# Older chunks first in three pipelined passes of a graph network, and half a copy less in its sort

## The chip, the cores and the metric

One core of a Trainium2 chip runs the whole program. The metric is the device time of one execution in microseconds (us); lower is better.

## The reference, cut to what matters

Two graph layers run over 100,000 nodes of 64 features and 25,000 edges (src, dst; sorted by dst). Between them and before them stands a layer norm. The second one has three rounds:

```python
for l in range(3):
    f1 = relu(x[row] @ nb_W[l] + nb_b[l])
    f2 = relu(x[col] @ self_W[l] + self_b[l])
    h = relu(concatenate([f1, f2], axis=1) @ att1_W[l] + att1_b[l])
    log_alpha = (h @ att2_W[l] + att2_b[l])[:, 0]
    mask = clip(sigmoid(log_alpha) * (ZETA - GAMMA) + GAMMA, 0.0, 1.0)
    rowsum = segment_sum(mask, row, num_segments=n) + 1e-06
    d_inv_sqrt = clip(rowsum ** (-0.5), 0.0, 10.0)
    vals = mask * d_inv_sqrt[row] * d_inv_sqrt[col]
    x = segment_sum(vals[:, None] * x[col], row, num_segments=n)
    out = out + x
```

Here row is src, col is dst, and x is the features of the nodes. The kernel needs the edges sorted by src as well, and so sorts 32,768 keys (two lists of edge ends, padded) itself.

## The kernel before, in words

**The sort** comes first. VectorE holds 128 x 512 keys and does a bitonic sort in 15 rounds. Each step is an `exchange`: one min (L1706) and one max (L1707) of 128x256 elements, from one buffer into the other. Rounds 9 to 15 also compare across partitions: TensorE turns the keys into a PSUM bank, VectorE copies all 512 columns back (L1716), exchanges, TensorE turns them again, and VectorE copies all 512 again (L1722). There are 14 such copies. Nothing else of the kernel can start before the sorted keys are stored.

**The second layer** works on 49 chunks of 512 edge slots, in three rounds (`l` = 0, 1, 2). Each round has first a pass that computes the attention of every edge and ends in the row sums, here called pass 1, 2 and 3, and then an aggregation. In a pass each chunk goes through these operations, on two engines whose queues run in program order:

- TensorE: turn (L1509 in pass 1, L1513 later), m1 (two products, L1523 and L1524), m2 (L1531, L1532), m3 (L1537), each waiting for ScalarE's result before it
- ScalarE: fill (copies of what was turned, L1431 and L1432), e2 (two Relus, L1437 and L1438), e3 (one Relu, L1445)

A helper, `staged`, writes the order out: at index i it calls each function for chunk i minus its lag, in the order of its list. After the pass ScalarE takes one sigmoid of 98x256 (L1449), VectorE works out the row sums (from L1313 on), and ScalarE takes a square root (L1451).

*Pass 1* has more in it. GpSimd (POOL) gathers both end rows of every edge by eight indirect DMAs a chunk (L1076) into two buffers; a buffer is free again once VectorE has passed `h_base`, at the end of the layer norm of the chunk that was in it. VectorE's norm of a chunk is: sum and centre (L570, L572), a square on ScalarE (L587), sum (L576), a root on ScalarE (L591), and scaling (L582, L1214). The square and the root are the first things in ScalarE's `fill` of this pass. Beside that, chunks 0 to 36 carry lookups: VectorE makes a one-hot (`above`, L1251), TensorE multiplies (`seek`, four groups of three L1490 and one L1492), VectorE selects the result of the lookup before (`found`, L1259). Every third chunk (2, 5, 8, ...) carries two lookups, the others one. `seek` is the last item in TensorE's list. At chunk 37 VectorE does a long piece, `place`.

*Passes 2 and 3* gather four rows a chunk (L1096). In them VectorE and ScalarE also take one step per chunk of a dense layer norm over all nodes (RUN_B, RUN_C): ScalarE's part is a square (L410) and a root (L415), VectorE's begins with L394, and SyncE loads and stores its rows. In the first 25 chunks VectorE also does two scans a chunk (L1239). After pass 3 VectorE waits until the last dense rows are stored (`run_stored`), and only then looks at the sigmoid. SyncE waits for the same stores at the end of `run_sp`, before it loads rows for the aggregation (`spread`, L1151).

Of the kernel before, what the change touches and what calls it, by code (L numbers as in the profile page):

```python
# [9 lines left out]
ALU = mybir.AluOpType  # L10
ACT = mybir.ActivationFunctionType
# [3 lines left out]
P = 128  # L15
# [31 lines left out]
NC1 = T1 // C  # L47
# [42 lines left out]
def build(nc, a, out):  # L90
    ctx = ExitStack()
    with ctx:
        def sb(name, shape, dt=F32):
            return ctx.enter_context(nc.sbuf_tensor(name, shape, dt))
# [168 lines left out]
        steps = sb("steps", [P, 256])  # L263
        row_of = sb("row_of", [P, 1])
        one_c = sb("one_c", [P, 1])
        perm1 = VAL1[:, :].bitcast(I32)
        rise = sb("rise", [RB1, 256])
        starts = sb("starts", [RB1, 1])
# [191 lines left out]
        def run_sp(sp, tag, src, dst):  # L460

            for c in range(DEPTH - 1):
                run_load(sp, tag, src, c)
            for c in range(len(tag[1])):
                run_store(sp, tag, dst, c)
                if c + DEPTH - 1 < len(tag[1]):
                    run_load(sp, tag, src, c + DEPTH - 1)
            run_stored(sp, tag)

        def run_stored(eng, tag):  # L470
            n = len(tag[1])
# [642 lines left out]
        def L1_sp(sp):  # L1114
# [31 lines left out]
            for l in range(LAYERS):  # L1146
                def spread(j, l=l):
                    b, c = j % 2, LOOKUPS[l][j]
                    if l or j >= 2:
                        sp.wait_ge(signal("o_hot"), LOOKUPS_BEFORE[l] + j - 1)  # L1150
                    sp.dma_start(RB[b], row_d[:, C * P * c:C * P * (c + 1)].broadcast_to([P, C * P])).then_inc(signal(f"o_ids{b}"), 16)  # L1151

                def store(c, l=l):
                    sp.wait_ge(signal("q_out"), l * NC1 + c + 1)
                    sp.dma_start(sums_of(xt_d[l], c), TS[:, c % 2]).then_inc(signal(f"q_stored{c % 2}"), 16)

                def load(c):
                    b = c % 3
                    if c >= 3:
                        sp.wait_ge(signal("q2_fin"), c - 2)  # L1160
                    sp.dma_start(LR[b][0].rearrange("p k f -> p (k f)"), base_d[c]).then_inc(signal(f"q2_ld{b}"), 16)
                    for n_ in range(2):
                        sp.dma_start(LR[b][1 + n_], sums_of(xt_d[n_], c)).then_inc(signal(f"q2_ld{b}"), 16)
                if l < 2:
                    for j in range(2):
                        spread(j)
                    sp.wait_ge(signal("r_val"), l + 1)
                    for h in range(2):
                        sp.dma_start(at(degree_d, 256 * h, [[512, COLS // 2], [1, 256]]), DEGR[h * (COLS // 2):(h + 1) * (COLS // 2)]).then_inc(signal("degrees_out"), 16)
                    due = looked_at(l, 3)  # L1170
                    staged(NC1, [(0, lambda i: [spread(j) for j in due(i) if j >= 2]), (5, store)])
                    for b in range(2):
                        sp.wait_ge(signal(f"q_stored{b}"), 16 * len(range(b, NC1, 2)) * (l + 1))
                    sp.sem_inc(signal("table"), 1)
                    run_sp(sp, (RUN_B, RUN_C)[l], x1_d, out)
                else:
                    for b in range(2):
                        sp.wait_ge(signal(f"h_stored{b}"), 16 * len(range(b, NC1, 2)))
                    staged(NC1, [(0, spread), (2, load)])

        def L1_dve(v):
            v.wait_ge(signal("x1_fixed"), 1)
# [46 lines left out]
            for l in range(LAYERS):  # L1229
                rowsum_dve(v, l)  # L1230
                aggregate_dve(v, l)
                if l < 2:
                    v.wait_ge(signal("s_bt"), NC1 * (l + 1))
                    v.wait_ge(signal("q_out"), NC1 * (l + 1))
                    for i in range(NC1):
# [3 lines left out]
                            v.tensor_tensor_scan(ownT[:, lo:hi][:, ::-1], sameB[:, lo + 1:hi + 1][:, ::-1], ownT[:, lo:hi][:, ::-1],  # L1239
                                                 ownT[:, hi:hi + 1] if c < NC1 - 1 else 0.0, ALU.mult, ALU.max).then_inc(signal("h_own"), 1)  # L1240
                        run_step(v, (RUN_B, RUN_C)[l], i)
                if l == 1:
                    run_stored(v, RUN_B)
                    run_stored(v, RUN_C)

        def above(v, e):

# [169 lines left out]
        def L1_act(s_):  # L1417

            for l in range(LAYERS):
# [24 lines left out]
                        s_.wait_ge(signal("h_m3"), l * NC1 + i - 1)  # L1444
                    s_.activation(HH[b], bank[4 + tb(l, i)][:, 0:256], ACT.Relu, bias=bias2[:, l:l + 1]).then_inc(signal("h_e3"), 1)  # L1445
                dense = [(0, lambda i, l=l: run_act_step(s_, (RUN_B, RUN_C)[l - 1], i))] if l else []
                staged(NC1, [(0, fill), (1, e2), (2, e3), *dense])
                s_.wait_ge(signal("h_m3"), (l + 1) * NC1)
                s_.activation(MR, bank[6][0:RB1, 0:256], ACT.Sigmoid, bias=bias3[0:RB1, l:l + 1]).then_inc(signal("r_sig"), 1)  # L1449
                s_.wait_ge(signal("r_total"), l + 1)  # L1450
# [20 lines left out]
        def L1_pe(pe):  # L1471
# [27 lines left out]
            for l in range(LAYERS):  # L1499
# [37 lines left out]
                    pe.matmul(bank[6][0:RB1, 0:256], at2[:, l, 48 - c:48 - c + RB1], HH[i % 2], start=(i == 0), stop=(i == NC1 - 1)).then_inc(signal("h_m3"), 1)  # L1537
                if l:
                    pe.wait_ge(signal("q_out"), l * NC1)
                staged(NC1, [(0, turn), (1, m1), (2, m2), (3, m3), *([] if l else [(0, seek)])])  # L1540

                pe.wait_ge(signal("r_ends"), l + 1)
                pe.matmul(bank[7][0:1, 0:RB1], PF[:, 255:256], ident[0:RB1, 0:RB1], start=True, stop=True)
# [102 lines left out]
        def _(v):  # L1646
# [55 lines left out]
            def exchange(cur, oth, d):  # L1702
# [4 lines left out]
                v.tensor_tensor(y[:, :, 1, :], x[:, :, 0, :], x[:, :, 1, :], ALU.max)  # L1707
                return oth, cur

            turns = 0  # L1710
            for k in range(1, 16):
                if k >= 9:
                    v.drain().then_inc(signal("turn_in"), 1)
                    turns += 1
                    v.wait_ge(signal("turned"), 2 * turns - 1)
                    v.tensor_copy(cur, bank[0][:, :])  # L1716
                    for st in range(k - 9, -1, -1):
                        cur, oth = exchange(cur, oth, 1 << st)
                    mid_side.append(0 if cur is KA else 1)
                    v.drain().then_inc(signal("turn_in"), 1)  # L1720
                    v.wait_ge(signal("turned"), 2 * turns)
                    v.tensor_copy(cur, bank[1][:, :])  # L1722
                for st in range(min(k, 8) - 1, -1, -1):
                    cur, oth = exchange(cur, oth, 1 << st)
                end_side.append(0 if cur is KA else 1)
                v.drain()
# [306 lines left out]
```

## Time and profile before

| | us |
|---|---|
| median of 3 executions (2831.07 to 2831.59) | 2831.31 |
| the profiled execution, device time | 2831.4 |
| its span, first to last instruction | 2829.6 |
| DVE (VectorE) busy | 2091.3 (74%) |
| POOL (GpSimd) busy | 1905.7 (67%) |
| PE (TensorE) busy | 1649.0 (58%) |
| ACT (ScalarE) busy | 1073.2 (38%) |
| mean granted TensorE clock | 0.768 of full |

Busy shares are averages over stages with different limits, so the stage of each edit has to be read by itself. The profiled execution lasts 1.8 us longer than its span, for what lies before the first instruction and after the last.

### The profile page before, as it was taken

How to read it: one execution, taken by the hardware profiler on the slowest of the kernel's cores; microseconds unless marked ns; L12 is line 12 of the kernel's file. 1: busy time of each engine (PE TensorE's matmuls, PEld its weight loads, DVE VectorE, ACT ScalarE, POOL GpSimd, SP SyncE). 2: the span in 40 equal slices, each digit the busy share in tenths (PEclk: the TensorE clock that was granted, in tenths of full speed). 3: DMA queues.
4: the chain of work that ended last, by engine and by line, in shares of the span. 5: the costliest groups of instructions: out<-in, count | busy, mean ns of one | idle time of the engine just before them, and what ended most of it. 6: DMA issues, size and time to landing. Idle time of an engine off the chain costs nothing.

```text
span 2829.6 us, 32874 instructions
## 1 busy us (share of the span) xinstructions
PE 1649.0 (58%) x8788; PEld 1262.0 (45%) x8788; DVE 2091.3 (74%) x5660; ACT 1073.2 (38%) x2214; POOL 1905.7 (67%) x1896
## 2 busy tenths in 40 slices
PE   1135667676508888256666546746666655656663
PEld 0025666666405555145454334534444444434442
DVE  6766998899778999355655536979668889657775
ACT  0025666666304443033333334434444344442221
POOL 0037777777786766677777774767766477745776
PEclk9997877877558888577777767878888778876555
DMA  0023444444201111422222112333323333324443
GB/s 8 0 60 92 137 129 138 129 139 127 84 2 32 45 43 41 87 59 66 61 62 64 41 35 56 85 99 105 103 91 74 86 102 105 104 68 120 126 116 81
DMA packets 279791, 226.66 MB, mean 80 GB/s; under 512 B 161731, under 2 KB 209855, under 8 KB 279481
## 3 DMA queue, kind: packets, MB, share of 16 engines
q1 hardware_dynamic: 221113, 184.48, 23.1%
q0 software_dynamic: 58496, 40.08, 6.8%
q8 instruction: 74, 1.21, 0.2%
q14 instruction: 108, 0.88, 0.1%
HBM read 151.81 MB, written 84.50 MB: 84 GB/s over the span
## 4 chain that ended last, share of the span: by engine, by line
POOL 48%; DVE 18%; issue 18%; PE 7%; DVEq 6%; DMA 2%; SPq 1%; ACT 1%; POOLq 0%; ACTq 0%
POOL big L1096 14%; POOL G L1076 13%; POOL regs L1973 7%; POOL out L1103 7%; POOL regs L1982 6%; DVE den L1377 2%; DVE big L1706 2%; PE bank L1562 2%; DVE bank L836 2%; DVE big L1394 2%; DVEq L1705 1%; PE bank L994 1%; DVE bank L847 1%; DVE G L830 1%; DVEq L837 1%
## 5 line engine op out<-in xcount | busy, mean ns | idle before, releaser
L1096 POOL DMA_INDIRECT big<-layer_rows,late x392 | 401.0, 1023 | 152.0 <-issue 118.8
L1973 POOL DMA_INDIRECT regs<-in_x,G x200 | 202.2, 1011 | 234.8 <-DVEq L1825 174.2
L1562 PE MATMUL bank<-regs,SQ 99*128 99x256 bf16 x1308 | 228.7, 345 | 84.7 <-ACT SQ L1467 78.1
L1103 POOL DMA_INDIRECT out<-G,scat_i x196 | 195.7, 999 | 104.3 <-issue 61.6
L1982 POOL DMA_INDIRECT regs<-in_x,G x200 | 220.1, 1101 | 65.4 <-issue 60.3
L685 POOL DMA_INDIRECT x_after_layer<-big,scat_i x200 | 196.5, 983 | 84.3 <-issue 65.7
L1076 POOL DMA_INDIRECT G<-x_after_layer,own_i x196 | 199.9, 1020 | 70.2 <-issue 60.7
L1076 POOL DMA_INDIRECT G<-x_after_layer,far_i x196 | 197.8, 1009 | 65.8 <-issue 65.8
L1064 POOL DMA_INDIRECT late<-degree_factors,late x152 | 152.8, 1005 | 99.9 <-DMA degree_factors<-den 56.6
L1562 PEld LDWEIGHTS bank<-regs,SQ 99*128 99x128 bf16 x1308 | 153.9, 121 | 144.7 <-ACT SQ L1467 97.0
L439 PE MATMUL bank<-regs 128*128 128x128 f32 x784 | 135.9, 327 | 119.4 <-DVE den L397 118.7
L1377 DVE SCALAR_TENSOR_TENSOR den<-steps,late,bank 128x256 f32<-128x256 f32 x436 | 182.0, 473 | 10.0 <-PE bank L1562 10.0
L439 PEld LDWEIGHTS bank<-regs 128*128 128x128 f32 x784 | 117.3, 230 | 135.4 <-issue 134.4
L1513 PE MATMUL bank<-ident,big 128*128 128x128 f32 x196 | 48.5, 337 | 217.4 <-DMA big<-layer_rows,late 217.4
L1509 PE MATMUL bank<-ident,XC 128*128 128x128 f32 x196 | 48.8, 398 | 211.1 <-DVEq L1215 211.1
L1465 ACT ACTIVATE SQ<-XC,row_of 128x512 bf16<-128x512 bf16 x109 | 78.4, 719 | 222.9 <-DMA XC<-row_of_far_degree 166.7
L587 ACT ACTIVATE SQ<-XC 128x512 f32<-128x512 f32 x99 | 62.3, 629 | 261.8 <-DVE XC L572 261.7
L527 PE MATMUL bank<-regs 128*128 128x196 bf16 x800 | 130.0, 307 | 27.6 <-DVE regs L543 24.2
L1997 POOL DMA_INDIRECT farf<-dst_float,VAL x96 | 122.4, 1275 | 29.2 <-issue 29.2
L1513 PEld LDWEIGHTS bank<-ident,big 128*128 128x128 f32 x196 | 22.5, 161 | 261.4 <-issue 261.4
L1509 PEld LDWEIGHTS bank<-ident,XC 128*128 128x128 f32 x196 | 32.1, 201 | 223.1 <-issue 223.1
L1524 PE MATMUL bank<-den,regs 128*128 128x256 f32 x294 | 127.4, 528 | 0.0
(417 smaller groups left out, 5384.6 us busy)
## 6 DMA issues: line engine op xcount, KB each, us to landing
den<-in_x SPq DMA_DIRECT2D x96, 256.0 KB, 3.7
x_after_layer<-den SPq DMA_DIRECT2D x96, 256.0 KB, 2.1
regs<-x_after_layer SPq DMA_DIRECT2D x96, 256.0 KB, 2.8
out<-regs SPq DMA_DIRECT2D x96, 256.0 KB, 2.1
XC<-row_of_far_degree SPq DMA_DIRECT2D x109, 128.0 KB
layer_rows<-TS SPq DMA_DIRECT2D x98, 128.0 KB
regs<-sought SPq DMA_DIRECT2D x49, 196.0 KB
regs<-row_of_edge SPq DMA_DIRECT2D x75, 128.0 KB
```

What stands on the lines that cost most here:

```text
L439: ins = pe.matmul(bank[(3, 6)[d % 2]][:, q * P:(q + 1) * P], XT[d % 2][:, q * P:(q + 1) * P], CM, start=True, stop=True)
L527: pe.matmul(o_, GE[b][h][:, k * P:(k + 1) * P], LT[:, h, part, :], start=(h + part == 0), stop=False)
L685: g.indirect_dma_start(x1_d, bass.IndirectOffsetOnAxis(ap=scat_i[0][:, u:u + 1], axis=0), big2[:, u, :], None, bounds_check=top, oob_is_er ...
L1064: g.indirect_dma_start(DCc[:, u:u + 1], None, degree_d, bass.IndirectOffsetOnAxis(ap=pos_i[:, u:u + 1], axis=0), bounds_check=top, oob_is_ ...
L1076: g.indirect_dma_start(G[:, b, grp // 2, grp % 2, :], None, x1_d, bass.IndirectOffsetOnAxis(ap=ix[:, u:u + 1], axis=0), bounds_check=top, ...
L1096: ahead(g, l, REVERSED, lambda u, l=l: g.indirect_dma_start(far[:, tile_of(u // C, u % C), :], None, xt_d[l - 1], bass.IndirectOffsetOnAxi ...
L1103: g.indirect_dma_start(out, bass.IndirectOffsetOnAxis(ap=scat_i[1][:, u:u + 1], axis=0), SUM[b][:, k, :], None, bounds_check=top, oob_is_e ...
L1377: v.scalar_tensor_tensor(PICK[k], steps[:, :], far_c[:, u:u + 1], bank[2 + 2 * (j % 2) + k // 2][:, (k % 2) * 256:(k % 2) * 256 + 256], AL ...
L1524: pe.matmul(bank[2 + b][:, 256:512], wb[:, 1, l, :], FT[b], start=True, stop=True).then_inc(signal("h_m1"), 1)
L1562: ins = pe.matmul(bank[2 + 2 * b + k // 2][:, (k % 2) * 256:(k % 2) * 256 + 256], OH[b][0:RB1 + 1, k * P:(k + 1) * P], TAB[0:RB1 + 1, part ...
L1973: g.indirect_dma_start(GR[:, c % DEEP, k, 0, :], None, a["x"], bass.IndirectOffsetOnAxis(ap=own0[:, c * C + k:c * C + k + 1], axis=0), bou ...
L1982: g.indirect_dma_start(GR[:, c % DEEP, k, 1, :], None, a["x"], bass.IndirectOffsetOnAxis(ap=far0[:, c * C + k:c * C + k + 1], axis=0), bou ...
```

## The change

Four edits. In the sort only the upper half of each turned pair is copied; the lower half is read by min and max in the PSUM bank. In the three passes TensorE's list becomes m3, m2, m1, turn and ScalarE's e3, e2 (in passes 2 and 3 then the dense step), fill; the lookup stays last on TensorE. At the last chunk ScalarE does a sigmoid on one column, so that the table for it is loaded there; in pass 1 after the fill, in passes 2 and 3 before it. VectorE's wait for the dense stores goes, and SyncE's moves behind the first two `spread` loads of the next aggregation.

```diff
@@ run_sp
                 if c + DEPTH - 1 < len(tag[1]):
                     run_load(sp, tag, src, c + DEPTH - 1)
-            run_stored(sp, tag)
@@ L1_sp
+                for j in range(2):
+                    spread(j)
+                if l:
+                    run_stored(sp, (RUN_B, RUN_C)[l - 1])
                 if l < 2:
-                    for j in range(2):
-                        spread(j)
...
-                    staged(NC1, [(0, spread), (2, load)])
+                    staged(NC1, [(0, lambda j: spread(j) if j >= 2 else None), (2, load)])
@@ L1_dve
-                if l == 1:
-                    run_stored(v, RUN_B)
-                    run_stored(v, RUN_C)
@@ L1_act
-                staged(NC1, [(0, fill), (1, e2), (2, e3), *dense])
+
+                def warm(i):
+                    if i == NC1 - 1:
+                        s_.activation(warm_c[:, :], one_c[:, :], ACT.Sigmoid)
+                staged(NC1, [(2, e3), (1, e2), *dense, *([(0, warm), (0, fill)] if l else [(0, fill), (0, warm)])])
@@ L1_pe
-                staged(NC1, [(0, turn), (1, m1), (2, m2), (3, m3), *([] if l else [(0, seek)])])
+                staged(NC1, [(3, m3), (2, m2), (1, m1), (0, turn), *([] if l else [(0, seek)])])
@@ block.vector, the sort
+            def exchange_turned(turned, cur, oth, d):
+                t_ = turned.rearrange("p (g t d) -> p g t d", t=2, d=d)
+                x = cur.rearrange("p (g t d) -> p g t d", t=2, d=d)
+                y = oth.rearrange("p (g t d) -> p g t d", t=2, d=d)
+                v.tensor_copy(x[:, :, 1, :], t_[:, :, 1, :])
+                v.drain()
+                v.tensor_tensor(y[:, :, 0, :], t_[:, :, 0, :], x[:, :, 1, :], ALU.min)
+                v.tensor_tensor(y[:, :, 1, :], t_[:, :, 0, :], x[:, :, 1, :], ALU.max)
+                return oth, cur
...
-                    v.tensor_copy(cur, bank[0][:, :])
-                    for st in range(k - 9, -1, -1):
+                    cur, oth = exchange_turned(bank[0][:, :], cur, oth, 1 << (k - 9))
+                    for st in range(k - 10, -1, -1):
...
-                    v.tensor_copy(cur, bank[1][:, :])
-                for st in range(min(k, 8) - 1, -1, -1):
+                    cur, oth = exchange_turned(bank[1][:, :], cur, oth, 1 << 7)
+                for st in range((min(k, 8) if k < 9 else 7) - 1, -1, -1):
```

## Rows read from the trace of the kernel before

**Rows 1.** The page's chain that ended last, shares of the span by source line.

```profile
POOL big L1096 14%; POOL G L1076 13%; POOL regs L1973 7%; POOL out L1103 7%; POOL regs L1982 6%; DVE den L1377 2%; DVE big L1706 2%; PE bank L1562 2%; DVE bank L836 2%; DVE big L1394 2%; DVEq L1705 1%; PE bank L994 1%; DVE bank L847 1%; DVE G L830 1%; DVEq L837 1%
```

**Rows 2.** Waits of POOL, 1185 to 1710 us (pass 1): total us, times, longest.

```profile
POOL G L1076 <- issue: 120.0, 374, 2.6
```

**Rows 3.** Timeline, pass 1: turns of chunks 0, 3, 37: start us, length us, what.

```profile
1191.55 1.09 PE L1509 MATMUL bank<-ident,XC 128*128 128x128 f32 x4 [6.01 <-DVEq L1215]
...
1220.93 0.75 PE L1509 MATMUL bank<-ident,XC 128*128 128x128 f32 x4 [3.87 <-DVEq L1215]
...
1582.50 0.63 PE L1509 MATMUL bank<-ident,XC 128*128 128x128 f32 x4 [3.59 <-DVEq L1215]
```

**Rows 4.** Timeline, pass 1: one step with two lookups (chunk 11) and the next turn.

```profile
1304.83 1.08 PE L1509 MATMUL bank<-ident,XC 128*128 128x128 f32 x4 [3.63 <-DVEq L1215]
...
1305.70 1.06 PE L1523 MATMUL bank<-big,regs 128*128 128x256 f32 x2
...
1306.05 0.08 DVE L1259 DVE_READ_ACCUMULATOR regs<-bank,late,steps 128x1 f32 x1
...
1307.66 0.47 ACT L1437 ACTIVATE den<-bank,bias 128x256 f32<-128x256 f32 x1 [1.05 <-PE bank L1524]
...
1312.53 0.69 DVE L570 TENSOR_REDUCE stat<-G 128x8 f32<-128x512 f32 x1
...
1314.03 0.63 ACT L587 ACTIVATE SQ<-XC 128x512 f32<-128x512 f32 x1 [4.19 <-DVE XC L572]
...
1317.41 1.09 PE L1509 MATMUL bank<-ident,XC 128*128 128x128 f32 x4 [3.87 <-DVEq L1215]
```

**Rows 5.** Stretch 1190 to 1320 us: engines' busy us, then granted clock, DMA share, GB/s.

```profile
1190.00:1320.00 130.00, 80.91 (x415) 63.79 (x416) 75.51 (x220) 39.09 (x95) 99.11 (x97) 0.72 0.26 66
```

**Rows 6.** Timeline, PE, pass 1: low clock in a lookup, twice; the earliest rise.

```profile
1192.43 0.84 PE L1490 MATMUL bank<-regs 98*128 98x256 bf16 x3
...
1418.49 0.84 PE L1490 MATMUL bank<-regs 98*128 98x256 bf16 x3
...
1490.80 0.69 PE L1531 MATMUL bank<-den,regs 128*128 128x256 f32 x2
```

**Rows 7.** Timeline, end of pass 1: from the last chunk's turn to the sigmoid's table.

```profile
1700.98 1.09 PE L1509 MATMUL bank<-ident,XC 128*128 128x128 f32 x4 [5.25 <-DVEq L1215]
...
1706.07 0.60 PE L1523 MATMUL bank<-big,regs 128*128 128x256 f32 x2
...
1706.94 0.60 PE L1531 MATMUL bank<-den,regs 128*128 128x256 f32 x2
1707.14 0.47 ACT L1437 ACTIVATE den<-bank,bias 128x256 f32<-128x256 f32 x1 [1.15 <-PE bank L1524]
...
1707.51 0.47 ACT L1438 ACTIVATE den<-bank,bias 128x256 f32<-128x256 f32 x1
...
1709.56 1.40 PE L1537 MATMUL bank<-den,regs 128*98 128x256 f32 x4
1709.76 0.47 ACT L1445 ACTIVATE den<-bank,bias 128x256 f32<-128x256 f32 x1 [1.28 <-PE bank L1532]
1710.25 1.28 ACT L1449 ACT_TABLE_LOAD   x1
```

**Rows 8.** Timeline, end of pass 3: last turn, sigmoid, first VectorE row behind its wait.

```profile
2522.43 0.41 PE L1513 MATMUL bank<-ident,big 128*128 128x128 f32 x2 [0.89 <-DMA big<-layer_rows,late]
...
2529.84 0.47 ACT L1449 ACTIVATE den<-bank,bias 98x256 f32<-98x256 f32 x1
...
2534.76 0.29 DVE L1313 TENSOR_SCALAR den<-den 98x256 f32<-98x256 f32 x1 [7.72 <-DMA out<-regs]
```

**Rows 9.** Groups of VectorE by shape: 512 copied out of a bank; 256 added from one.

```profile
L853 DVE TENSOR_TENSOR big<-bank,big 128x256 f32<-128x256 f32 x50 | 20.4, 408 | 1.8 <-PE bank L1003 1.8
...
L1716 DVE COPY big<-bank 128x512 f32<-128x512 f32 x7 | 4.8, 692 | 8.7 <-PE bank L1914 8.7
```

**Rows 10.** Waits of all engines, 1990 to 2112 us (second half of pass 2).

```profile
DVE bank L394 <- ACT dstat L415: 34.7, 24, 3.1
```

More of the change, by code:

```diff
@@ L265, in build @@
         one_c = sb("one_c", [P, 1])
+        warm_c = sb("warm_c", [P, 1])
         perm1 = VAL1[:, :].bitcast(I32)
```

## The prediction

> **What bounds the kernel now.** I read the page first, for the chain that ended last [rows 1]. GpSimd's indirect DMAs head it, one line per stage; the 13% of L1076 are pass 1. So I asked stage by stage whether GpSimd is ever held up. In pass 1 it is not: 374 of its idle stretches are the 0.32 us between two issues [rows 2]. Then I read the timeline of pass 1, step by step. From the turn of chunk 3 to that of chunk 37 there are 34 steps in 361.6 us, 10.63 us each [rows 3], which is the pace of eight gathers. Last I read the three ends of the passes and the sort, where no gather runs and each microsecond counts in full.
>
> **The sort.** Each of 14 full copies from a bank takes 0.69 us [rows 9]. A 256-wide operation that reads a bank takes 0.41 us, so I price the half copy at that: 0.28 us less. The min and max now read one operand in the bank; 0.41 us for such an add [rows 9] says that this costs nothing. The sort has no cover and nothing beside it, so 14 x 0.28 = **-3.9 us**. Bounds: 0, if reading the bank made min and max slower by as much together, and 14 x 0.35 = 4.9 if a half copy took half.
>
> **The end of pass 1.** Before: the last turn starts at 1700.98, then come m1, m2, m3 of chunks 47, 46, 45, and only then m1 of 48 at 1706.07; the sigmoid is ready to start at 1711.5, behind its table load [rows 7]. New: the turn is followed by m3 of 46, m2 of 47 and m1 of 48. At the low clock m3 takes 0.85 and m1 and m2 1.71 each, twice the 0.87 from L1523 to L1531 at the high one [rows 7]. So m1 of 48 starts at 1704.4. The low clock lasts until about 1706. L1437 starts 1.96 us after L1523 at the low clock [rows 4], 1.07 at the high one [rows 7]: 1706.4. e2 takes 0.84 (L1437 start to L1438 end), m2 to e3 1.07, e3 0.47, and m3 after e3 0.73 (1710.96 minus 1710.23) [rows 7]. That gives 1709.5 for the sigmoid: **-2.0 us**. The table load (1.28 us, rows 7) now lies between fill and e3 of 47, where ScalarE waits for m2 until 1704.7.
>
> **The end of pass 2** has the same rows as pass 3 and no wait of VectorE; the same count gives **-1.6 us**. Its load lies before the last fill. It is covered if ScalarE's dense step 48 is done 1.6 us (load and one column) before the last gather lands. Now VectorE waits for ScalarE in 24 steps of the second half of pass 2 [rows 10], since that dense step stands behind e3, which hangs on the gather; in the new order it comes right after e2 of the chunk before, so I expect it to be early. Without cover it costs up to 2.1 us.
>
> **The end of pass 3.** The last turn is at 2522.43 and the sigmoid at 2529.84, but VectorE starts at 2534.76, since it waits for the store [rows 8]. New, by the same terms and all at the high clock: m3, m2 and m1 of 48 start at 2522.7, 2523.1, 2524.0; L1437 2525.1, end of e2 2525.9, e3 2527.0, m3, sigmoid 2528.2, VectorE 2528.7. That is **-6.0 us**. SyncE's wait for the stores stays, but its first final load comes only after ScalarE's first one-hot, some 9 us later, so nothing new is late.
>
> On table loads the Trainium skill ("ScalarE: Activation LUTs", What ACT_TABLE_LOAD costs) gives 2.66 us a switch, drain included. The trace shows 1.28 us and then the sigmoid. By the page's figure the gains at the ends would still hold, as the loads are covered either way.
>
> **Pass 1 under the new order.** This is where I expect the loss. ScalarE's queue now has e3 and e2 ahead of fill, and fill begins with the norm's square for the chunk that has just landed. e2 of chunk c waits for m1 of c, and in TensorE's queue m1 of c stands behind m3, m2, and these behind the lookup of chunk c. Before, all this came after the fill, and the lookup behind everything. So now a closed loop runs from turn to turn: turn, lookup, m3, m2, m1, e2, square, rest of the norm, next turn. If it is longer than 10.63 us, GpSimd waits for `h_base`.
>
> Its terms, from the turn's start: the lookup starts when VectorE has the first half of the result before, at 1306.13 minus 1304.83 = 1.3, plus 0.15, so 1.45. A lookup is four groups; at the low clock one takes 0.69 (four end 2.8 us after the first start, of which rows 6 have one), at the high one 0.35. m3 and m2 before m1: 2.56 low, 1.30 high. From m1's start to the square: 1.07 + 0.86 = 1.93 high, 2.82 low. From the square to the next turn: 1317.41 minus 1314.03 = 3.38 [rows 4].
>
> The granted clock in this stretch is 0.72 [rows 5]: 1.2 GHz in part of each step, 2.4 in the rest. In the 34 steps it rose between 2.7 us (L1531 at 1490.80, turn at 1488.21) and 5.9 us (L1490 still low at 1418.49, turn at 1413.34) after the turn [rows 6], 4.35 in the mean. TensorE idles about as long per step in the new order (4.4 us against 3.9), so I keep this mean. One lookup: 1.45 + 2.76 = 4.21, then m3 and m2 almost all at the high clock, m1 at 5.6, square at 7.5, **10.9 us**. Two lookups: the halves of the first end at 2.8 and 4.2, and VectorE's selection takes 0.8 for each, until 5.1; the second half of the second lookup waits for that, starts at 5.25 and ends at 5.95, m1 at 7.25, square at 9.2, **12.55 us**. The old step with two lookups took as long, 12.58 [rows 4], since VectorE started L570 only at 7.7; but the steps with one made it good again, and now they can't.
>
> Sum over the 34 steps: 23 x 10.9 + 11 x 12.55 = 388.8, against 361.6: +27.2. At the start, chunk 1 has no gather to wait for: its lookup starts 0.88 us after the turn [rows 3, 6], ends at 3.65, m1 follows at the low clock (2.82) and then the 3.38, so its turn comes 9.85 us after chunk 0's at 1191.55; then 10.9 and 12.55 give 1224.85 for chunk 3, against 1220.93: +3.9. GpSimd is 4.3 us ahead of the loop at most, and `place` at chunk 37, during which it already is held up a little, takes that slack away. So **+31 us**, carried to the end. Chunks 38 to 48 have no lookup; their loop is at most 9.6 us and hides.
>
> A rule of the skill speaks the same way ("TensorE: Matmul & The Clock Gate", Step-by-step: what each phase is for): matmuls stay in program order. Were it otherwise, m1 could pass a lookup and the gathers would still set the pace.
>
> **Passes 2 and 3 in the middle.** The loop fill, m1, e2, dense square and root, fill is 0.4 + 1.96 + 0.84 + 0.9 = 4.1 us at the low clock, under the four gathers' 5.3. Nothing.
>
> **The sum**, against the profiled execution's 2831.4 (the median is 2831.3): -3.9 - 2.0 - 1.6 - 6.0 + 31 = +17.5, so 2849.
>
> **The rivals.**
> - *The loop hides* (0.22). If TensorE were at the high clock all through, one lookup gives 9.4 us and two 11.5, 30.3 for three steps against 31.9 of gathers, and only the gains are left: 2818. With the earliest rise everywhere (10.15, 12.05) three steps take 32.35 and it is about 2826. The point that decides is 31.9 us for three steps. Against it: the clock was low at the start of nearly every step, with the same idle time before it.
> - *The dense steps hold up the fill in passes 2 and 3 too* (0.08). In the first half VectorE's step has two scans more and goes at about the gathers' pace. If ScalarE waited in each of 98 steps 0.3 us more than the gathers allow, that is 29 us more: 2878.
> - *The sigmoid's table does not stay* (0.04). If each Relu behind it needed another, three loads of 1.28 us come in at each end, and the gains there shrink by some 4 us: 2853. Now Relu and Copy run after Exp and after Sqrt without one.
>
> **How the numbers follow.** The forecast (0.66) is 2849, its own range 2836 to 2864: a mean rise half a microsecond earlier or later moves a step by 0.25 to 0.3 us, the sum by 10. The range of 8 in 10 has to take in the first rival: 2817 to 2864. A difference under 0.2%, 5.7 us, can't be told from none here. Slower: 0.66 and the last two rivals, less the low end: 0.71. Within 0.2%: 0.08. Faster: 0.21.
>
> **What would show it.** In the changed profile GpSimd's L1076 would wait for L1214 in most chunks up to 37, about 31 us in sum, where it now waits only for issue; L587 would start right behind L1438; turns with one lookup would be 10.9 us apart. The 14 copies would take 0.41 us. No table load stands before L1449's sigmoid, and VectorE starts 0.5 us after it in all passes. The prediction is wrong if the distance of turns in pass 1 stays at 10.6.

## The result, and the profile after

| | before | after |
|---|---|---|
| median of 4 executions, us | 2831.19 | 2904.26 |
| lowest to highest, us | 2830.83 to 2831.59 | 2900.53 to 2905.36 |
| ratio, 95% interval | | 1.0256 (1.0240 to 1.0271) |
| span of the profiled execution, us | 2829.6 | 2903.5 |
| mean granted TensorE clock | 0.768 | 0.753 |

The change costs 73 us. The forecast was slower by 18 us, in a range that ended at 2864. So the sign was right, and the size wrong by 55 us. The places of the 73.9 us between the two spans, in order of time: the sort -4.0, layer 0 +7.4, pass 1 from first to last gather +72.7 (530.7 us before, 603.5 after), from there to VectorE's first row of the row sums -3.2, passes 2 and 3 +1.4, the rest -0.5.

Lines have moved by up to four: after, the turn is L1512 (later L1516), the lookup L1493, m1 L1526, m2 L1534, m3 L1540; e2 is L1436 and L1437, e3 L1444; `h_base` is L1216, the sigmoid L1452, VectorE's first row of the row sums L1312.

**Pass 1.** The waits of GpSimd over the whole span, after:

```profile
POOL G L1076 <- issue: 112.0, 354, 1.9
POOL G L1076 <- DVE VS L1216: 101.4, 38, 8.7
```

The same view of the kernel before:

```profile
POOL G L1076 <- issue: 126.5, 390, 2.6
POOL G L1076 <- DVE VS L1214: 9.5, 2, 8.3
```

GpSimd now waits for a free buffer 38 times, once in nearly every chunk up to 37. That is 91.9 us more of waiting; 14.5 us of it only take the place of time between issues (126.5 to 112.0). The turns of chunks 0, 3 and 37 in the timeline after answer to [rows 3]:

```profile
1195.37 1.09 PE L1512 MATMUL bank<-ident,XC 128*128 128x128 f32 x4 [6.02 <-DVEq L1217]
...
1231.91 1.09 PE L1512 MATMUL bank<-ident,XC 128*128 128x128 f32 x4 [4.15 <-DVEq L1217]
...
1658.30 1.09 PE L1512 MATMUL bank<-ident,XC 128*128 128x128 f32 x4 [4.15 <-DVEq L1217]
```

From chunk 3 to 37 it is 426.4 us, where before it was 361.6 and the forecast 388.8. From chunk 0 to 3 it is 36.5 us, before 29.4, forecast 33.3. Now one step, chunk 9, with one lookup:

```profile
1307.92 0.63 PE L1512 MATMUL bank<-ident,XC 128*128 128x128 f32 x4 [4.15 <-DVEq L1217]
1308.00 0.99 POOL L1076 DMA_INDIRECT G<-x_after_layer,own_i  x1 [3.80 <-DVE VS L1216]
...
1309.40 0.80 PE L1493 MATMUL bank<-regs 98*128 98x256 bf16 x3 [0.86 <-DVE regs L1258]
...
1312.07 1.15 PE L1540 MATMUL bank<-den,regs 128*98 128x256 f32 x2
...
1313.02 1.06 PE L1534 MATMUL bank<-den,regs 128*128 128x256 f32 x2
...
1314.72 1.04 PE L1526 MATMUL bank<-big,regs 128*128 128x256 f32 x2
...
1316.61 0.47 ACT L1437 ACTIVATE den<-bank,bias 128x256 f32<-128x256 f32 x1
1316.96 0.63 ACT L587 ACTIVATE SQ<-XC 128x512 f32<-128x512 f32 x1
...
1320.35 1.09 PE L1512 MATMUL bank<-ident,XC 128*128 128x128 f32 x4 [4.15 <-DVEq L1217]
1320.42 0.99 POOL L1076 DMA_INDIRECT G<-x_after_layer,own_i  x1 [2.33 <-DVE VS L1216]
```

These rows are the loop of the forecast, link by link: turn, lookup, m3, m2, m1, e2, square right behind L1437, next turn, and a gather 0.07 to 0.08 us behind each turn. Everything from the lookup to m1's first product runs at the low clock: 0.80 us for a group of the lookup, 1.04 to 1.15 for a product's row. The granted clock of the stretch, which answers to [rows 5]:

```profile
1190.00:1320.00 130.00, 78.62 (x340) 56.13 (x340) 62.60 (x175) 33.78 (x82) 79.93 (x80) 0.66 0.23 55
```

It is 0.66 instead of 0.72, so a larger part of each step lies at 1.2 GHz. The steps don't scatter: from chunk 10 to 36 they repeat, within 0.02 us, three lengths.

| step | turn to m1 | m1 to square | square to turn | step | forecast |
|---|---|---|---|---|---|
| two lookups (chunk 11, 14, ...) | 8.66 | 1.79 | 3.38 | 13.83 | 12.55 |
| one lookup, behind it | 6.80 | 2.21 | 3.38 | 12.39 (chunk 9: 12.43) | 10.9 |
| one lookup, the next | 6.17 | 1.79 | 3.38 | 11.34 | 10.9 |

Three steps take 37.55 us, where the forecast had 34.35 and the gathers need 31.9.

**The ends of the passes.** The end of pass 1 after, which answers to [rows 7]:

```profile
1777.04 1.09 PE L1512 MATMUL bank<-ident,XC 128*128 128x128 f32 x4 [6.23 <-DVEq L1217]
...
1778.84 1.28 ACT L1449 ACT_TABLE_LOAD   x1
...
1784.53 0.47 ACT L1452 ACTIVATE den<-bank,bias 98x256 f32<-98x256 f32 x1 [0.77 <-PE bank L1540]
...
1785.11 0.29 DVE L1312 TENSOR_SCALAR den<-den 98x256 f32<-98x256 f32 x1 [8.26 <-ACT den L1452]
```

From the last turn to VectorE it is 8.1 us, before 11.1: -3.1. At the end of pass 2, from the issue of the last gather to VectorE, it is 9.5 us (2184.49 to 2193.96), before 11.9 (2110.03 to 2121.97): -2.5. The end of pass 3 answers to [rows 8]:

```profile
2593.51 3.05 SPq L457 DMA_DIRECT2D out<-regs  x2
2593.53 1.00 POOL L1096 DMA_INDIRECT big<-layer_rows,late  x1 [0.30 <-issue]
...
2596.60 0.94 SPq L1151 DMA_DIRECT2D XC<-row_of_far_degree  x2
...
2600.40 0.66 PE L1516 MATMUL bank<-ident,big 128*128 128x128 f32 x2 [6.97 <-DMA big<-layer_rows,late]
...
2608.66 0.47 ACT L1452 ACTIVATE den<-bank,bias 98x256 f32<-98x256 f32 x1 [0.77 <-PE bank L1540]
2609.17 0.29 DVE L1312 TENSOR_SCALAR den<-den 98x256 f32<-98x256 f32 x1 [12.90 <-ACT den L1452]
```

VectorE starts 0.5 us after the sigmoid, as forecast, and no table load stands before it. But the last gather's data reach TensorE 5.9 us after the gather's end on GpSimd (2594.53 to 2600.40). In the kernel before it was 1.4 us:

```profile
2520.01 1.00 POOL L1096 DMA_INDIRECT big<-layer_rows,late  x1 [0.30 <-issue]
...
2523.71 3.62 SPq L456 DMA_DIRECT2D out<-regs  x2
```

There, the last two dense stores were issued after that gather had landed; now the first of them goes 0.02 us ahead of it. Each of the two is a tail, a short block of 106 partitions, 212 KB. (The row at 2593.51 stands for both; the second is issued at 2596.30, 1.8 us after the gather's end.) From the issue of the last gather to VectorE it is 15.6 us, before 14.8.

**The sort.** Groups of VectorE by shape, after (answers to [rows 9]):

```profile
L1719 DVE TENSOR_TENSOR big<-bank,big 128x256 f32<-128x256 f32 x14 | 5.9, 425 | 1.0
L1717 DVE COPY big<-bank 128x256 f32<-128x256 f32 x14 | 5.9, 424 | 17.3 <-PE bank L1927 8.7 <-PE bank L1932 8.7
...
L1720 DVE TENSOR_TENSOR big<-bank,big 128x256 f32<-128x256 f32 x14 | 5.8, 415 | 0.0
```

The half copy takes 0.42 us, and min and max with an operand in the bank (0.425 and 0.415) take what those without one take (0.425 and 0.418). The first gather behind the sort is issued at 174.2 us, before at 178.2.

### The profile page after: what moved, and what is told of

It is laid out like the page before. It is cut to its first block, busy times and chain, and to the rows that moved or that the text cites. A ratio compares the mean times of both kernels' runs of the same rounds, so it can differ in the third digit from the quotient of the medians.

```text
span 2903.5 us, 32871 instructions
## 1 busy us (share of the span) xinstructions
PE 1703.7 (59%) x8788; PEld 1276.0 (44%) x8788; DVE 2088.1 (72%) x5660; ACT 1067.9 (37%) x2217; POOL 1905.7 (66%) x1896
## 4 chain that ended last, share of the span: by engine, by line
POOL 36%; DVE 21%; PE 16%; issue 15%; DVEq 6%; ACT 3%; DMA 2%; SPq 1%; POOLq 0%; ACTq 0%
POOL big L1096 14%; POOL regs L1986 7%; POOL out L1103 7%; POOL regs L1995 6%; PE bank L1493 5%; POOL G L1076 2%; DVE den L1376 2%; PE bank L1565 2%; DVE big L1709 2%; DVE bank L836 2%; PE bank L1540 1%; DVE big L1393 1%; PE bank L994 1%; DVE XC L582 1%; DVEq L1708 1%
## 5 line engine op out<-in xcount | busy, mean ns | idle before, releaser
L1565 PE MATMUL bank<-regs,SQ 99*128 99x256 bf16 x1308 | 233.3, 350 | 79.7 <-ACT SQ L1470 73.9
L576 DVE TENSOR_REDUCE stat<-SQ 128x8 f32<-128x512 f32 x99 | 67.5, 682 | 209.3 <-ACT SQ L587 209.3
L1444 ACT ACTIVATE den<-bank,bias 128x256 f32<-128x256 f32 x147 | 69.6, 473 | 337.8 <-PE bank L1535 337.7
L1512 PE MATMUL bank<-ident,XC 128*128 128x128 f32 x196 | 43.7, 364 | 225.1 <-DVEq L1217 225.1
L1516 PE MATMUL bank<-ident,big 128*128 128x128 f32 x196 | 48.7, 338 | 205.2 <-DMA big<-layer_rows,late 205.0
L1493 PE MATMUL bank<-regs 98*128 98x256 bf16 x588 | 135.6, 405 | 23.9 <-DVE regs L1258 23.9
L1512 PEld LDWEIGHTS bank<-ident,XC 128*128 128x128 f32 x196 | 28.9, 185 | 245.1 <-issue 245.1
```

The costliest lines, as they stand in the source:

```text
L1493: pe.matmul(bank[5 + 2 * h][:, (k % 2) * 256:(k % 2 + 1) * 256], GEQ[e % 2][:, k * P:(k + 1) * P], RISE[:, part * 256:(part + 1) * 256], s ...
L1565: ins = pe.matmul(bank[2 + 2 * b + k // 2][:, (k % 2) * 256:(k % 2) * 256 + 256], OH[b][0:RB1 + 1, k * P:(k + 1) * P], TAB[0:RB1 + 1, part ...
```

## The experiments

The rivals were: the loss of pass 1 comes from ScalarE's list (fill last), from TensorE's list, from both together, or from the clock in the loop; and, for the lost gain at the end of pass 3, from the tail stores, from any store there, or from the loads moved ahead. In the diffs below the list in pass 1 is the `else` of `if l`. The ratio of each run is estimated from all its executions, and need not be the quotient of the two medians.

**Four kernels on a chip where everything took 1000 us more** (e1, e2, e3, e4). The kernel before took 3861.6 us there, and the DMA engines moved 58 to 59 GB/s in the mean in the four profiles, not 80. The edits are those of e1b, e2b, e3b and e4b below. With gathers this slow, a few microseconds say nothing about the kernel elsewhere.

> The changed kernel with the old lists of both engines in pass 1 only. Theory of the closed loop (turn, lookup, m1, e2, square, turn): the gathers set the pace again, pass 1 is back at about 531 us from first to last gather, GpSimd waits for the norm under 12 us, and only the gains at the ends are left: 2815 to 2822 us. Rival, that the new order of passes 2 and 3 or the moved wait for the stores costs as well: above 2835 us.

> The changed kernel with ScalarE's old list in pass 1 (fill before e2 and e3), TensorE's list as changed, m1 still behind the lookup. Theory of the closed loop: ScalarE's square no longer stands behind e2, so the loop is open and the time is that of the kernel with both old lists, within 4 us. Rival, that TensorE's list alone does the harm (m's late behind lookups): near 2904 us.

> The changed kernel with nine extra float32 products of 128x256 in each step of pass 1, on TensorE between m1 and the next turn, where it idled for 4.15 us; their result is overwritten by the turn and nothing reads it. Theory that the loop was mis-sized by TensorE's clock: the granted clock of pass 1 goes from 0.70 to 0.9 or more, a step with one lookup takes 9.4 to 10 us and one with two 11.5 to 12, the gathers set the pace again, and the time is 2815 to 2835 us. Rival, that other terms of the loop are longer than counted and the clock hardly matters: steps stay above 11 and 12.5 us, 2860 us or more.

> The kernel before with the sort's edit alone. If the gain on the path is carried to the end: 3.9 us less, 2827 us. Rival: the first gather starts 4 us earlier but the layer between, which TensorE's clock paces in part, gives it back, as the trace of the changed kernel suggests (L685 ends 3.4 us later in it): 2830 to 2835 us.

Measured: 1.0005 (0.9969 to 1.0041), 0.9998 (0.9960 to 1.0035), 1.0110 (1.0071 to 1.0148) and 0.9956 (0.9911 to 1.0001). The first two and the fourth can't be told from no change. The changed kernel itself did not run there, and why the third was 1.1% slower was not followed up; the four edits were run again on other chips.

**Pass 1's lists as before, all else changed** (e1b).

```diff
- staged(NC1, [(2, e3), (1, e2), *dense, *([(0, warm), (0, fill)] if l else [(0, fill), (0, warm)])])
+ staged(NC1, [(2, e3), (1, e2), *dense, (0, warm), (0, fill)] if l else [(0, fill), (0, warm), (1, e2), (2, e3)])
- staged(NC1, [(3, m3), (2, m2), (1, m1), (0, turn), *([] if l else [(0, seek)])])
+ staged(NC1, [(3, m3), (2, m2), (1, m1), (0, turn)] if l else [(0, turn), (1, m1), (2, m2), (3, m3), (0, seek)])
```

> The changed kernel with the old lists of both engines in pass 1 only, again, since on the chip of the first four runs every kernel took about 1000 us more. Theory of the closed loop (turn, lookup, m1, e2, square, turn): pass 1 is back at about 531 us from first to last gather, GpSimd waits for the norm under 12 us, and only the gains at the ends are left: 2815 to 2822 us where the kernel before takes 2831. Rival, that the new order of passes 2 and 3 or the moved wait for the stores costs as well: above 2835 us.

Measured: 2832.84 against 2833.63, 1.0000 (0.9989 to 1.0012). GpSimd's waits:

```profile
POOL G L1076 <- issue: 126.6, 390, 2.5
POOL G L1076 <- DVE VS L1216: 9.7, 2, 8.5
```

The whole loss is gone with the two lists of pass 1. But the gain that was expected does not show either (2815 to 2822 us expected), and the timeline of the end of pass 3 shows one reason:

```profile
2521.45 3.26 SPq L457 DMA_DIRECT2D out<-regs  x2
2521.65 1.00 POOL L1096 DMA_INDIRECT big<-layer_rows,late  x1 [0.31 <-issue]
...
2528.34 0.66 PE L1516 MATMUL bank<-ident,big 128*128 128x128 f32 x2 [6.75 <-DMA big<-layer_rows,late]
...
2536.47 0.29 DVE L1312 TENSOR_SCALAR den<-den 98x256 f32<-98x256 f32 x1 [12.04 <-ACT den L1452]
```

Again the first tail store goes just ahead of the last gather, and the gather's data reach TensorE 5.7 us after its end (2522.65 to 2528.34).

**The new lists in pass 1 alone, in the kernel before** (e5).

```diff
- staged(NC1, [(0, fill), (1, e2), (2, e3), *dense])
+ staged(NC1, [(0, fill), (1, e2), (2, e3), *dense] if l else [(2, e3), (1, e2), (0, fill)])
- staged(NC1, [(0, turn), (1, m1), (2, m2), (3, m3), *([] if l else [(0, seek)])])
+ staged(NC1, [(0, turn), (1, m1), (2, m2), (3, m3)] if l else [(3, m3), (2, m2), (1, m1), (0, turn), (0, seek)])
```

> The kernel before with the new lists in pass 1 alone. Theory of the closed loop: all of the harm, 70 to 80 us more than before; turns repeat every three steps in about 37.5 us against 31.9. Rival, that part of the harm needs the other edits: under 60 us more.

Measured: 2902.65 (2 executions) against 2834.03, 1.0242 (1.0217 to 1.0266). GpSimd waits 38 times for L1214, 100.3 us, and the steps show the same three lengths, 11.33, 13.83 and 12.39. So these two lines alone make the loss.

**ScalarE's list of pass 1 as before, TensorE's new** (e2b). The edit is the first pair of lines of e1b's diff.

> The changed kernel with ScalarE's old list in pass 1 and TensorE's as changed, again, on a chip where the kernel before takes about 2831 us. Theory of the closed loop: the square no longer stands behind e2, so the time is that of the kernel with both old lists in pass 1 (equal to before within 3 us). Rival, that m1 behind the lookup is harm by itself: above 2850 us.

Measured: 2832.34 against 2830.89, 1.0006 (0.9993 to 1.0020). GpSimd waits for L1216 twice, 10.1 us, and the turns of chunks 3 and 37 lie 364.4 us apart. TensorE's new list without ScalarE's does no harm: the square then does not stand behind e2.

The same trace bears on the end of pass 3. Its lists there are the new ones and its loads are moved too, but the first tail store happens to go out 0.2 us after the last gather's end on GpSimd:

```profile
2524.84 0.99 POOL L1096 DMA_INDIRECT big<-layer_rows,late  x1 [0.30 <-issue]
...
2526.01 2.96 SPq L457 DMA_DIRECT2D out<-regs  x2
...
2527.37 0.41 PE L1516 MATMUL bank<-ident,big 128*128 128x128 f32 x2 [1.70 <-DMA big<-layer_rows,late]
...
2533.78 0.29 DVE L1312 TENSOR_SCALAR den<-den 98x256 f32<-98x256 f32 x1 [5.09 <-ACT den L1452]
```

The data are there 1.5 us after the gather's end, so neither the new order nor the moved loads delay them by themselves. From the turn to VectorE it is 6.4 us, all at the high clock, and from the gather's issue 8.9 us, before 14.8. In e11 and e3b, below, that store goes 1.15 us ahead of the gather's issue, and the data come 5.0 and 5.1 us after its end.

**The lookup behind m1** (e11). It comes behind m1 of the same chunk and ahead of the next turn; ScalarE's list stays new.

```diff
- staged(NC1, [(3, m3), (2, m2), (1, m1), (0, turn), *([] if l else [(0, seek)])])
+ staged(NC1, [(3, m3), (2, m2), (1, m1), *([] if l else [(1, seek)]), (0, turn)])
```

> The changed kernel with the lookup of a chunk moved in TensorE's list of pass 1 behind m1 of the same chunk, so that it lies in the wait before the next turn; ScalarE's list stays as changed. Theory that the loop is too long by the lookup: what is left of it, turn, m3, m2, m1, e2, square and norm, is at most 9.6 us, the gathers set the pace, and the time is 2815 to 2835 us. Rival, that e2 and e3 ahead of the square are enough for the harm: above 2860 us.

Measured: 2827.42 against 2830.89, 0.9989 (0.9976 to 1.0002). GpSimd waits for L1216 twice, 9.8 us. The granted clock of 1190 to 1320 us is 0.74. So ScalarE's new list does no harm either, once the lookup does not stand between the turn and m1. It takes both: the square behind e2, and the lookup ahead of m1.

**Nine more products on TensorE in each step of pass 1** (e3b). Their result is overwritten; no part of the computation is left out.

```diff
+ def busy(i):
+     if i:
+         for _ in range(9):
+             pe.matmul(bank[0][:, 0:256], ident[:, :], steps[:, :], start=True, stop=True)
- staged(NC1, [(3, m3), (2, m2), (1, m1), (0, turn), *([] if l else [(0, seek)])])
+ staged(NC1, [(3, m3), (2, m2), (1, m1), *([] if l else [(0, busy)]), (0, turn), *([] if l else [(0, seek)])])
```

> The changed kernel with nine extra float32 products of 128x256 in each step of pass 1, on TensorE between m1 and the next turn, again. Theory that the loop was mis-sized by TensorE's clock: the granted clock of pass 1 goes from 0.70 to above 0.8, a step with one lookup takes about 10 us and one with two 12, and the time falls to 2815 to 2850 us. Rival, that other terms of the loop are longer than counted and the clock hardly matters: steps stay above 11 and 12.5 us, 2870 us or more.

Measured: 2830.98 against 2833.63, 0.9990 (0.9975 to 1.0004): with both new lists and more work on TensorE, the loss is gone. One step of it, chunk 4, on TensorE:

```profile
1225.83 0.63 PE L1512 MATMUL bank<-ident,XC 128*128 128x128 f32 x4 [0.27 <-DVEq L1217]
...
1227.29 0.49 PE L1493 MATMUL bank<-regs 98*128 98x256 bf16 x3 [0.83 <-DVE regs L1258]
...
1228.72 0.65 PE L1540 MATMUL bank<-den,regs 128*98 128x256 f32 x2
...
1230.08 0.59 PE L1526 MATMUL bank<-big,regs 128*128 128x256 f32 x2
...
1230.94 4.05 PE L1547 MATMUL bank<-steps,ident 128*128 128x256 f32 x18
1235.25 0.63 PE L1512 MATMUL bank<-ident,XC 128*128 128x128 f32 x4 [0.26 <-DVEq L1217]
```

and the granted clock of three stretches of the pass (last figures but two of each row):

```profile
1190.00:1320.00 130.00, 114.40 (x658) 93.78 (x659) 75.42 (x219) 40.34 (x100) 98.31 (x98) 0.96 0.26 62
1320.00:1450.00 130.00, 112.79 (x644) 91.52 (x642) 74.73 (x218) 38.57 (x96) 99.01 (x98) 0.95 0.26 63
1450.00:1560.00 110.00, 95.01 (x533) 76.68 (x532) 62.45 (x180) 32.85 (x82) 82.33 (x81) 0.94 0.26 60
```

m1 starts 4.25 us after the turn, not 6.17 to 6.80, and this step takes 9.42 us. Most steps with one lookup take 9.42 to 9.50, four of the eleven with two take 11.44 to 11.50: the forecast's 9.4 and 11.5 for the high clock. Five times the clock fell (chunks 8, 14, 17, 26, 29), and those steps took 13.1 to 15.3 us; the short steps between made it good again. The turns of chunks 3 and 37 lie 364.0 us apart, and GpSimd waits 4 times. So it is the clock that makes this loop longer than the gathers.

**The sort's edit alone, in the kernel before** (e4b). The edit is the block `exchange_turned` of the change and its three calls.

> The kernel before with the sort's edit alone, again, since the first run was on the chip where all took 1000 us more. If the gain on the path is carried to the end: 4 us less than before. Rival: it is given back in the layer between: within 2 us of before.

Measured: 2828.39 against 2834.03, 0.9987 (0.9975 to 0.9999), which is -3.7 us in an interval 7 us wide.

**The waits' edit alone, in the kernel before** (e7). VectorE's two `run_stored` go, and SyncE's stands behind its first two `spread`.

> The kernel before with the waits' edit alone (VectorE's wait for the dense stores gone, SyncE's moved behind the first two loads). Theory that the end of pass 3 gave nothing in the changed kernel because the new order puts the last two dense stores in front of the last gather, which then lands 5.9 us after its issue instead of 1.4: with the old order the stores stay behind the gather, VectorE starts right after the sigmoid, and the time is 4.5 us less than before. Rival, that the moved loads themselves disturb the last gather: no gain, and the last turn of pass 3 late here too.

Measured: 2828.16 against 2834.03, 0.9984 (0.9971 to 0.9997), or -4.5 us. In the timeline of the end of pass 3 the stores are issued after the last turn, as in the kernel before, and VectorE starts 7.9 us after that turn, before 12.3:

```profile
2518.58 0.41 PE L1511 MATMUL bank<-ident,big 128*128 128x128 f32 x2 [0.90 <-DMA big<-layer_rows,late]
...
2520.27 3.21 SPq L456 DMA_DIRECT2D out<-regs  x2
```

**Tail stores first** (e10). To the kernel with pass 1's old lists, one line: the two dense blocks of 106 partitions are the first of pass 3, no longer the last.

```diff
- RUN_IDS = [[*range(DCH + 2)], [*range(49)], [*range(49, DCH + 2)]]
+ RUN_IDS = [[*range(DCH + 2)], [*range(49)], [DCH, DCH + 1, *range(49, DCH)]]
```

> The changed kernel with the old lists in pass 1, and the two short blocks of the dense run in pass 3 (106 partitions) taken first instead of last. Theory that their stores hold up the last gather of pass 3: its last turn follows the last issue's end by 1.4 to 2.5 us instead of 5.7, and the time is 4 to 5 us less than with the short blocks last, 12 to 15 us under the kernel before. Rival, that any store there does it, or the loads moved ahead: the last turn stays 5 to 6 us late and the time is that of the kernel before, within 3 us.

Measured: 2824.64 against 2830.89, 0.9970 (0.9956 to 0.9983). The end of pass 3:

```profile
2517.33 0.33 SPq L459 DMA_DIRECT2D out<-regs  x1
2517.36 1.00 POOL L1096 DMA_INDIRECT big<-layer_rows,late  x1 [0.31 <-issue]
...
2520.02 0.66 PE L1516 MATMUL bank<-ident,big 128*128 128x128 f32 x2 [2.68 <-DMA big<-layer_rows,late]
...
2528.07 0.29 DVE L1312 TENSOR_SCALAR den<-den 98x256 f32<-98x256 f32 x1 [7.89 <-ACT den L1452]
```

The last gather's data are there 1.7 us after its end, and from its issue to VectorE it is 10.7 us; in e1b, with the tails last, 14.8. And yet a store stands 0.03 us ahead of this gather too: one of a full block, 128 partitions and 256 KB. So it is not any store that delays the gather, but the short ones. How the DMA engines are used differs as well. The changed kernel just after the gather's end, and this one at the same place (last three figures: granted clock, DMA share, GB/s):

```profile
2594.60:2596.30 1.70, 0.00 (x0) 0.00 (x0) 1.52 (x3) 1.40 (x2) 0.00 (x0) 0.80 0.13 30
...
2518.00:2520.00 2.00, 0.00 (x0) 0.01 (x1) 1.41 (x3) 1.90 (x4) 0.36 (x1) 0.99 0.39 135
```

A share of 0.13 of 16 engines is the work of about two (an estimate). That the gather's data wait behind the store on those few is argued, not shown. The whole time fell by less than the expected 12 to 15 us: by the ratio it is 8.5.

**New lists in pass 2 only** (e9) and **all lists as before** (e8). The sort, the waits and, in pass 1, the early table stay changed:

```diff
- staged(NC1, [(2, e3), (1, e2), *dense, *([(0, warm), (0, fill)] if l else [(0, fill), (0, warm)])])
+ staged(NC1, [(0, fill), (1, e2), (2, e3), *dense] if l else [(0, fill), (0, warm), (1, e2), (2, e3)])
- staged(NC1, [(3, m3), (2, m2), (1, m1), (0, turn), *([] if l else [(0, seek)])])
+ staged(NC1, [(0, turn), (1, m1), (2, m2), (3, m3), *([] if l else [(0, seek)])])
```

This is e8's diff; e9 keeps the new lists where l is 1.

> The changed kernel with the old lists in passes 1 and 3 and the new ones in pass 2 only. In the trace with new lists in passes 2 and 3 the end of pass 2 (last gather's issue to VectorE's start) took 9.4 us instead of 11.9, so 2.5 us less than with all lists old: about 12 us under the kernel before. Rival: the time between single runs hides it.

> The changed kernel with the old lists in all three passes; the sort's edit, the waits' edit and the early table in pass 1 stay. If the gains add up: 4.0 for the sort, 4.5 for the wait, 0.5 for the table, so 9 us under the kernel before. If the sort's gain is given back in the layer between: 5 us under it.

Measured: new lists in pass 2 only 2825.15 against 2830.89, 0.9978 (0.9966 to 0.9990); all lists old 2824.07 against 2834.03, 0.9958 (0.9943 to 0.9973). From the issue of the last gather of pass 3 to VectorE it is 10.4 us in the first and 12.0 in the second. The second is the fastest version of all; its interval meets those of the first and of the version with the tails first, so a gain from the new lists in any pass is not shown. By its ratio e8 is 12 us under the kernel before, more than the 9 expected; e9 is 6 us under it, half of the 12 expected, though the end of its pass 2 takes 9.5 us, as foreseen.

## Why the prediction was right or wrong

**The sort: right.** -3.9 forecast, 4.0 us earlier at the first gather, and -3.7 by its own run.

**The mechanism of pass 1: right.** A loop from turn to turn, too long for the gathers, seen in GpSimd's wait for `h_base` in nearly every chunk up to 37 and in the square right behind L1437. e5 shows that the two lists of pass 1 alone make the loss, e2b and e11 that it takes both links: the square behind e2, and the lookup between turn and m1. The loop of chunks 38 to 48 hides, as forecast.

**The size of pass 1: wrong, and this is the step that failed.** "TensorE idles about as long per step in the new order (4.4 us against 3.9), so I keep this mean": the mean rise of the clock at 4.35 us after the turn, taken from the old order. In the new one the first row wholly at the high clock starts 5.7, 7.65 or 7.76 us after the turn in the steps from chunk 9 to 36, 7.0 in the mean, so that every lookup lies at the low clock in full. Term by term: turn to m1 5.6 forecast, 6.17 and 6.80 measured; with two lookups 7.25 and 8.66. The other terms hold (3.38 to the next turn; m1 to square 1.93 forecast, 1.79 or 2.21). So a step with one lookup was 10.9 in the forecast and is 11.34 or 12.4, one with two was 12.55 and is 13.83. Over the 34 steps this makes 426.4 - 388.8 = 37.6 us more than forecast, and the first three steps another 3.2. The own range, half a microsecond on either side of the mean, priced the scatter of the old steps and not a shift of all of them. What fixes the time of the rise within a step was not found: the same three lengths came in two kernels, but no run varied the idle time in small steps. In the old order the turns followed the gathers' pace; in the new one they follow the chain that the clock itself lengthens. It is argued, not shown, that this is why the steps lock.

The Trainium skill ("TensorE: Matmul & The Clock Gate", HAM oscillation — how this bites in real kernels) tells of a loop in which a wait in each iteration makes TensorE start each iteration cold again. The trace agrees: 4.15 us of idle time before each turn and the low clock behind it, and 0.94 to 0.96 once the idle time is filled.

**The end of pass 3: wrong.** -6.0 forecast, +0.9 in the changed kernel. From turn to VectorE the forecast had 6.3 us, all at the high clock; it took 8.8, since behind the longer wait m1 ran at the low clock, and 8.1 in e10. That is some 2.5 of the 6.9 us missed; the step that failed is the other 4.5. There the sum took from before, without saying so, that the last gather lands as it did. The dense steps come earlier in the new order, as the prediction said for pass 2, and so the first tail store goes out just ahead of the last gather. That gather was then late by 4.5 us (5.9 less 1.4). In e10 the delay is gone, and in e7, which has the old lists, it never came. The second store and the moved loads come 1.8 and 2.1 us after the gather's end, when the data of an undelayed gather (1.4 to 1.7 us) have landed, so they can't have begun the delay. In e2b, where the store came after the gather, the forecast holds: 6.4 us from turn to VectorE for 6.3, and -5.8 us for -6.0 counted from the gather's issue. So the sum holds where the gather lands in time and TensorE's wait before the last turn is short (1.70 us in e2b; behind 2.68 us in e10 m1 began at the low clock). Which of the two goes first was settled by about a microsecond either way.

**The ends of passes 1 and 2: a little better than forecast.** -3.1 for -2.0 and -2.5 for -1.6. The sigmoid's table stays, as forecast, since Relu runs on with it: the four rows of e3 and e2 between L1449 and L1452 have no load before them. That is what the Trainium skill says ("ScalarE: Activation LUTs", Table sets: the hidden batching unit): cheap functions such as Relu are in every set. In pass 2 the load is not quite covered: it starts 0.2 us after the last turn, but TensorE, with m3 and m2 to do, waits only 0.3 us for the fill.

**Passes 2 and 3 in the middle: right as far as can be seen, but not shown to be nothing.** From VectorE's first row of the row sums in pass 1 (L1312, before L1313) to that in pass 2 it is 408.9 us, before 409.9. From the first gather of pass 3 to its last it is 261.5 us, before 259.7. The profiles of the other kernels, one execution each, hint at a cost that the forecast put at nothing. With the new lists and the tails last pass 3's gathers take 260.2 to 263.3 us, with the old lists 257.0 to 260.6; in pass 2 it is 258.9 to 262.2 against 256.3 to 258.7. But e10, with the new lists and the tails first, has 258.1 and 258.8. GpSimd is not held up in any of them, only its gathers last longer in the mean (1.03 to 1.04 us against 1.02). No run was made for it, and the cause stays open. Some 2 us in each pass would take back a good part of what the ends give. The expectation that ScalarE's dense step would be early in pass 2 was not borne out in VectorE's waits: 34.2 us in 23 waits for L416, before 34.7 in 24 [rows 10].

**Layer 0: no term.** The first gather of pass 1 is 3.4 us later after a sort that ends 4.0 earlier. The change touches nothing there. In e1b, with the same sort, that gather comes at 1158.0, 4.7 earlier than before. The granted clock of 875 to 1150 us was 0.84 before, 0.82 after and 0.89 in e1b. So this is taken for what one execution differs from another, which no run tested; it is about as much as each of the small gains, and why a sum against one profiled execution can't be closed to a few microseconds.

## What to carry to other kernels

Before a software pipeline is reordered, draw the loop through both engines' queues with all that stands ahead on each, and compare it with the pace of what should set the time; what harmed here was what then stood between, the lookup ahead of m1 and e2 ahead of the square, and either alone did nothing. Price each link of such a loop at the low clock if the engine idles in each round: a forecast with the old order's mean rise of the clock gave 31 us where it was 73. And where work ends earlier, ask what it releases: here a short store that now went out just ahead of the last gather took the gain back.

## What was not expected of the hardware

- With an idle time of 4.15 us before each turn, the granted clock rose at fixed places of three steps, which repeated for 27 chunks to 0.02 us, in two different kernels. Nine more products a step, 4.05 us of work in that idle time, raised the granted clock from 0.66 to 0.96 and made the pass 62 us shorter from chunk 3 to 37 (426.4 to 364.0).
- A store of 106 partitions issued 0.02 to 1.15 us ahead of a gather made the gather's data arrive 5.0 to 5.9 us after its end on GpSimd, instead of 1.4 to 1.7. A store of 128 partitions 0.03 us ahead did not, nor did one of 106 partitions issued 0.2 us after the gather's end. How it delays them was not tried.
- One chip ran all five kernels tried there, the kernel before among them, 1000 us slower; its four profiles show 58 to 59 GB/s.
